# The probabilities of the first attention turned by VectorE and by transfers through DRAM, and its value product one iteration later

## The reference

```python
q_hk = (hidden_q @ Wq.T).reshape(b, s, H, K)
q_big = einsum('bshk,hkq->bshq', q_hk, w_kc_q)
kv_rope = kv_c * cos + rotate_half(kv_c) * sin
q_r = einsum('bshq,hqr->bhsr', q_big, W_qr)
k_r = einsum('bld,hdr->bhlr', kv_rope, W_kr)
attn = softmax(einsum('bhsr,bhlr->bhsl', q_r, k_r))
ctx_c = einsum('bhsl,bld->bhsd', attn, kv_rope)
ctx_lat = einsum('bhsd,hkd->bshk', ctx_c, w_kc_kv)
out = ctx_lat.reshape(b, s, H * K) @ Wo.T
x = x + tanh(g_xattn[0]) * out
```

## Time and profile before

| | |
|---|---|
| median of 3 runs | 1411.74 us (1410.79 to 1411.82) |
| the profiled execution | 1410.01 us |
| its span on the core | 1408.2 us |
| TensorE busy | 98% of the span |
| VectorE, ScalarE, GpSimd busy | 62%, 37%, 29% |
| transposes of `Pb` on TensorE | 256, from 41.7 to 461.4 us |

### The profile page before, as it was taken

One profiled execution on the slowest core, in us unless ns is written; L12 is line 12 of the kernel. 1 busy time (PEld: TensorE's weight loads), 2 busy tenths in 40 slices (PEclk: granted clock), 3 DMA queues, 4 the chain that ended last, 5 costly groups with the idle time before them and its releaser, 6 DMA issues.

```text
span 1408.2 us, 20791 instructions
## 1 busy us (share of the span) xinstructions
PE 1384.4 (98%) x7948; PEld 1128.5 (80%) x7948; DVE 874.9 (62%) x1729; ACT 519.2 (37%) x1599; POOL 404.9 (29%) x463
## 2 busy tenths in 40 slices
PE   6999999999999999999999999999999999999999
PEld 5888888888887788878887888778887788887887
DVE  5455454455554687777677757776788787734443
ACT  2544444444355322131113211321126777822221
POOL 3112322222224444111121112113527865621000
PEclk9999999999999999999999999999999999999999
DMA  5432010110203221111011101111214131132111
GB/s 202 150 108 89 33 66 8 53 39 8 83 24 94 86 74 56 47 31 49 23 38 42 46 17 48 41 45 49 79 50 141 49 128 61 47 113 67 53 46 45
DMA packets 65127, 89.07 MB, mean 63 GB/s; under 512 B 8044, under 2 KB 31724, under 8 KB 65028
## 3 DMA queue, kind: packets, MB, share of 16 engines
q1 hardware_dynamic: 65028, 87.74, 19.5%
HBM read 70.94 MB, written 16.78 MB: 62 GB/s over the span
## 4 chain that ended last, share of the span: by engine, by line
PE 92%; DVE 4%; POOL 1%; ACT 1%; DMA 1%; issue 0%; SPq 0%; DVEq 0%; ACTq 0%; POOLq 0%
PE bank L118 86%; PE bank L121 7%; DVE STG L130 0%; DVE AH L130 0%; DVE st L152 0%; DVE XR L140 0%; DMA STG<-in_WoT_dram 0%; DVE sm L146 0%; DMA XR<-in_x_dram 0%; ACT Pb L124 0%; ACT STG L124 0%; DVE XR L137 0%; POOL XR L137 0%; POOL P L130 0%; DVE MSK L136 0%
## 5 line engine op out<-in xcount | busy, mean ns | idle before, releaser
L118 PE MATMUL bank<-XT,AR 128*128 128x512 f32 x1152 | 280.2, 393 | 0.3 <-DVE AR L130 0.2
L118 PE MATMUL bank<-AR 128*128 128x512 f32 x1056 | 261.5, 397 | 0.9 <-DVE PTV L127 0.7
L118 PEld LDWEIGHTS bank<-XT,AR 128*128 128x128 f32 x1152 | 213.8, 188 | 48.5 <-issue 1.5
L118 PEld LDWEIGHTS bank<-AR 128*128 128x128 f32 x1056 | 193.4, 188 | 46.9 <-DVE PTV L140 2.5
L124 ACT ACTIVATE STG<-bank,b1c 128x512 f32<-128x512 f32 x128 | 88.4, 691 | 379.1 <-PE bank L118 300.6
L118 PE MATMUL bank<-AR,CT 128*128 128x512 f32 x768 | 190.3, 397 | 0.0
L118 PE MATMUL bank<-AR,AH 128*128 128x512 f32 x768 | 187.5, 391 | 0.0
L118 PEld LDWEIGHTS bank<-AR,AH 128*128 128x128 f32 x768 | 143.1, 188 | 30.3 <-issue 1.1
L118 PEld LDWEIGHTS bank<-AR,CT 128*128 128x128 f32 x768 | 142.7, 189 | 30.0 <-issue 0.4
L127 DVE CAST AH<-STG 128x512 fp32r<-128x512 f32 x192 | 91.0, 474 | 118.7 <-PE bank L118 104.4
L127 POOL CAST BA<-STG 128x256 fp32r<-128x256 f32 x64 | 29.6, 463 | 420.7 <-PE bank L118 312.5
(11 more groups left out here) (132 smaller groups left out, 1881.0 us busy)
## 6 DMA issues: line engine op xcount, KB each, us to landing
XR<-scr SPq DMA_DIRECT2D x52, 256.0 KB, 2.8
XR<-in_x_dram SPq DMA_DIRECT2D x32, 256.0 KB, 4.2
scr<-XR SPq DMA_DIRECT2D x32, 256.0 KB, 2.0
STG<-in_Wq_dram SPq DMA_DIRECT2D x8, 512.0 KB, 3.4
STG<-in_WoT_dram SPq DMA_DIRECT2D x8, 512.0 KB, 5.4
STG<-in_W1L_dram SPq DMA_DIRECT2D x16, 256.0 KB, 2.6
STG<-in_W_dram SPq DMA_DIRECT2D x16, 256.0 KB, 2.7
STG<-in_B1T_dram SPq DMA_DIRECT2D x64, 64.0 KB, 1.9
```

What stands on the lines that cost most here:

```text
L118: return self.e.matmul(o, w, x, start=start, stop=stop, skip_group_check=True) if self.e else Nothing()
```

## The change

For units 0 to 29 (`by_dma`), P is no longer turned by TensorE. VectorE transposes each 32 by 32 block of `Pb` within its own strip of 32 partitions and writes the blocks to `PY`, grouped by their place among the four block columns of a tile (`blocks1`, two instructions, ending in `py_ok`). SyncE stores `PY` to DRAM (`p_store`, 512 KB) and reads it back with rows and block columns exchanged in four transfers of 128 KB, in rows of 1 KB, into `PZ` (`p_load`). `split1p` makes the high part (ScalarE, one instruction of 1024 columns) and the low part (VectorE, one instruction, `pz_ok`) of `PT`. `PY` and `PZ` share their space with `TM`, which is used later.

The value product of a unit and both halves of its output product come one iteration later, up to iteration 31. Units 30 and 31 are still turned by TensorE, and the iterations 31 to 34 are written out so that the loop ends as before. The stores of x, `final1` and `kv_split` move one iteration back accordingly, and the four loads of x tiles per block are spread over p = 2, 3 and 4. In SyncE's queue `p_store(u - 2)` stands ahead of the weights' loads of iteration u and `p_load(u - 2)` behind them.

```diff
--- before.py
+++ after.py
@@ -159,6 +159,9 @@
         return self.e.max_index(o, m, x) if self.e else Nothing()
+
+    def turn(self, o, x):
+        return self.e.transpose(o, x) if self.e else Nothing()
     def memset(self, o, v):
@@ -223,6 +226,8 @@
         w12c = sb("w12c", [128, 2, 4], F32)
+        with ExitStack() as st1:
+            PYZ = sb("PYZ", [128, 2, 1024], F32, st1)
         TM = sb("TM", [128, 4, 512], FR, st12)
@@ -263,6 +268,7 @@
               for p in range(8)]
+        PY, PZ = PYZ[:, 0, :], PYZ[:, 1, :]
         sWq, sKq, sKc, sWo, sWr = STG[:, 0:1024], STG[:, 1024:1792], STG[:, 1792:2048], STG[:, 2048:3072], STG[:, 3072:3456]
@@ -295,6 +301,7 @@
         scr = [nc.dram_tensor(f"scr{k}", [NT, D], F32, kind="Internal").ap() for k in range(3)]
+        pscr = [nc.dram_tensor(f"pscr{k}", [128, 1024], F32, kind="Internal").ap() for k in range(2)]
         xs = [i["x"], scr[0], scr[1], scr[2], out]
@@ -326,6 +333,7 @@
         t_x4 = [sig(f"t_x4{k}", 16) for k in range(8)]
+        t_py, d_pz = sig("t_py", 16), sig("d_pz", 16)
         def kinds(count, names):
@@ -335,6 +343,7 @@
         ms2_ok, tl_ok2, tl_sum, al_in, ix_ok = kinds(on_dve, "ms2_ok tl_ok2 tl_sum al_in ix_ok")
+        py_ok, pz_ok = kinds(on_dve, "py_ok pz_ok")
         c_mh, c_sel, rs_ok, kvc_rd, kvr_ok, kvl_ok = kinds(on_pool, "c_mh c_sel rs_ok kvc_rd kvr_ok kvl_ok")
@@ -409,6 +418,17 @@
             return t_xf[tb][m]
+
+
+
+        def by_dma(u):
+            return u < 30
+
+        def blocks_in(t):
+            return t.rearrange("p (n i c) -> p n i c", i=4, c=32)
+
+        def blocks_out(t):
+            return t.rearrange("p (i n c) -> p n i c", i=4, c=32)
         def ct_read(u, half):
@@ -607,8 +627,11 @@
                     pe.wait_ge(*ps.free(key))
-                    pe.wait_ge(*ps.drained(("pt", u, 0)))
-                    pe.wait_ge(*ps.drained(("pt", u, 1)))
+                    if by_dma(u):
+                        pe.wait_ge(*pz_ok[u])
+                    else:
+                        pe.wait_ge(*ps.drained(("pt", u, 0)))
+                        pe.wait_ge(*ps.drained(("pt", u, 1)))
                     pe.wait_ge(*kvl_ok[m])
@@ -764,22 +787,35 @@
                     k1(u)
-                if u >= 3:
-                    wo1(u - 3, 1)
+                if 4 <= u < NU:
+                    wo1(u - 4, 1)
                 if u + 1 < 8:
                     prep_b(u + 1)
-                if 2 <= u <= NU + 1:
-                    pv1(u - 2)
+                if 3 <= u < NU:
+                    pv1(u - 3)
                 if u < NU and p == 7 and m + 1 < NM:
                     kv_turn(m + 1)
                 if u < NU and 3 <= p <= 6:
                     ln_turn(*after1(m), p - 3, ring4.next())
-                if 1 <= u <= NU:
-                    turn1(u - 1)
+                if 3 <= u < NU:
+                    wo1(u - 3, 0)
+                if u == 31:
+                    wo1(28, 1)
+                    pv1(29)
+                    turn1(30)
+                if u == 32:
+                    wo1(29, 0)
+                    wo1(29, 1)
+                    pv1(30)
+                    turn1(31)
+                    wo1(30, 0)
                 if u == 33:
+                    wo1(30, 1)
+                    pv1(31)
                     stA0(0)
-                if 2 <= u <= NU + 1:
-                    wo1(u - 2, 0)
+                    wo1(31, 0)
+                if u == 34:
+                    wo1(31, 1)
                 if u == 33:
@@ -1086,7 +1122,7 @@
                     if u:
-                        ac.wait_ge(*ps.full(("pt", u - 1, j)))
+                        ac.wait_ge(*(py_ok[u - 1, j] if by_dma(u - 1) else ps.full(("pt", u - 1, j))))
                     elif j == 0:
@@ -1108,6 +1144,13 @@
                     hi_of(key, CT[:, 512 * half:512 * half + 512], ps.ap(key)[:, :])
+
+            def split1p(u):
+                key = "pz", u
+                ac.wait_ge(*d_pz[u, 3])
+                if u:
+                    ac.wait_ge(*ps.full(("pv", u - 1, 1)))
+                hi_of(key, blocks_in(PT[:, 0:1024]), blocks_out(PZ))
             def turn1(u):
@@ -1188,13 +1231,19 @@
                     prep_b(u + 1)
-                if 2 <= u <= NU + 1:
-                    pv1(u - 2)
+                if 3 <= u < NU:
+                    pv1(u - 3)
                 if u < NU and p == 7 and m + 1 < NM:
                     kv_turn(m + 1)
                 if u < NU and 3 <= p <= 6:
                     ln_turn(*after1(m), p - 3)
-                if 1 <= u <= NU:
+                if 2 <= u < NU:
+                    split1p(u - 2)
+                if u == 31:
+                    pv1(29)
+                if u in (32, 33):
+                    pv1(u - 2)
+                if u in (31, 32):
                     turn1(u - 1)
@@ -1468,6 +1517,16 @@
                     lo_of(key, lo, ps.ap(key)[:, :], hi).then_inc(*ps.drain(key, on_dve))
+            def blocks1(u):
+                for j in range(2):
+                    e.wait_ge(*nm_ok[u, j])
+                    if u:
+                        e.wait_ge(*t_py[u - 1])
+                    e.turn(blocks_out(PY)[:, 4 * j:4 * j + 4], blocks_in(Pb)[:, 4 * j:4 * j + 4]).then_inc(*py_ok.mark((u, j)))
+
+            def split1p(u):
+                lo_of(("pz", u), blocks_in(PT[:, 1024:2048]), blocks_out(PZ), blocks_in(PT[:, 0:1024])).then_inc(*pz_ok.mark(u))
+
             def turn1(u):
@@ -1576,29 +1635,40 @@
                     k1(u)
-                if u >= 3 and (u - 3) % 8 == 7:
-                    final1((u - 3) // 8, 2)
-                    final1((u - 3) // 8, 3)
+                if 4 <= u < NU and (u - 4) % 8 == 7:
+                    final1((u - 4) // 8, 2)
+                    final1((u - 4) // 8, 3)
+                if u == 34:
+                    final1(3, 2)
+                    final1(3, 3)
                 if u + 1 < 8:
                     prep_b(u + 1)
-                if 2 <= u <= NU:
-                    pv1(u - 2)
+                if 3 <= u < NU:
+                    pv1(u - 3)
                 if u < NU and p == 7 and m + 1 < NM:
                     kv_turn(m + 1)
                 if u < NU and 3 <= p <= 6:
                     ln_turn(*after1(m), p - 3)
                 if u < NU and 2 <= p <= 5:
                     ln_pre(*after1(m), p - 2)
-                if 1 <= u <= NU:
+                if 2 <= u < NU:
+                    split1p(u - 2)
+                if 1 <= u < 31:
+                    blocks1(u - 1)
+                if u in (31, 32):
+                    pv1(u - 2)
                     turn1(u - 1)
                 if u == 33:
                     mask_turn(0)
                     masks_a(0)
                 if u == 34:
                     masks_b(0)
-                if 2 <= u <= NU + 1 and (u - 2) % 8 == 7:
-                    final1((u - 2) // 8, 0)
-                    final1((u - 2) // 8, 1)
+                if 3 <= u < NU and (u - 3) % 8 == 7:
+                    final1((u - 3) // 8, 0)
+                    final1((u - 3) // 8, 1)
+                if u == 33:
+                    final1(3, 0)
+                    final1(3, 1)
                 if u == 32:
@@ -1969,8 +2039,8 @@
                     norm1(u - 1)
-                if 2 <= u <= NU + 1 and (u - 2) % 8 == 7 and (u - 2) // 8 + 1 < NM:
-                    kv_split((u - 2) // 8 + 1)
+                if 3 <= u < NU and (u - 3) % 8 == 7 and (u - 3) // 8 + 1 < NM:
+                    kv_split((u - 3) // 8 + 1)
                 if u < NU and 2 <= p <= 5:
@@ -2081,6 +2151,20 @@
                 e.dma(sWo, i["WoT"][p]).then_inc(*d_Wo.mark(p))
+            def p_store(u):
+                e.wait_ge(*py_ok[u, 1])
+                if u >= 2:
+                    e.wait_ge(*d_pz[u - 2, 3])
+                e.dma(pscr[u % 2], PY).then_inc(*t_py.mark(u))
+
+            def p_load(u):
+                e.wait_ge(*t_py[u])
+                if u:
+                    e.wait_ge(*pz_ok[u - 1])
+                src = pscr[u % 2].rearrange("(j r) (i x) -> i r j x", j=4, i=4)
+                for k in range(4):
+                    e.dma(PZ[32 * k:32 * k + 32, :].rearrange("r (j x) -> r j x", j=4), src[k]).then_inc(*d_pz.mark((u, k)))
+
             def kv_load(m):
@@ -2121,18 +2205,21 @@
                 m, p = divmod(u, 8)
+                if 2 <= u < NU:
+                    p_store(u - 2)
                 if u + 1 < 8:
                     prep_a(u + 1)
                     prep_b(u + 1)
+                if 2 <= u < NU:
+                    p_load(u - 2)
                 if u >= 32:
                     ba_load(u - 32)
-                if u >= 3 and (u - 3) % 8 == 7 and u < NU:
+                if u < NU and 2 <= p <= 4:
+                    for tb in ((0,), (1, 2), (3,))[p - 2]:
+                        ln_load(*after1(m), tb)
+                if u >= 4 and (u - 4) % 8 == 7 and u < NU:
                     for b in (2, 3):
```

(10 more changed lines are left out.)

## The result

The changed kernel takes 1457.4 us (median of 4 runs, 1455.4 to 1459.9) against 1411.8 before: a ratio of 1.0321 [1.0301, 1.0342], slower. The profiled execution took 1455.4 us with a span of 1453.6, so 45.4 us more of span than before. The forecast was 1458.1.

A forecast was written before the change was run, and what follows sets the result against it. TensorE, busy 98% of the span, was taken to bound the kernel. The loop's -7.0, stalls of +43.9 and slower pace of +9.5 made +46.4 us: a median of 1458.1 us against 1411.7, range 1440 to 1474.

The forecast's parts named there:

- The stalls: TensorE waits five times, u = 2 to 6, for weights' loads queued behind the store of P; 43.9 us in all.
- L: Time from the issue of P's store to the landing of Wqr; taken as 5.8 us, a similar train having taken 6.15.
- My sign of waits of 8 to 11 us: TensorE's timeline would show five such waits ahead of `prep_a`'s 12 products, with 20 products after each at twice their time.
- nothing: In SyncE's queue, the loads of P behind `prep_b`'s loads have the long iteration and were to cost no time.
- The slow pace: TensorE at its slower clock after each stall: half of the start's 3.84 us, 1.9 us each, 9.5 in all.
- The eviction: TensorE waits for the value product's eviction, 0.85 us in bare iterations, 0.41 with another turn; 16.3 us come back.
- Turns, copy and difference: Per unit, VectorE's two block turns 1.4 us, ScalarE's copy 1.1 us and VectorE's difference 1.5 us.
- Its rival: P's round trip through DRAM becomes the bound, 0.8 us over in 24 iterations, +19 us: 1477; chance 0.13.
- The 0.8 us in iterations 11, 19 and 27: VectorE's sums of the residual make TensorE wait 0.8 us in each of these iterations, +2.4 us.
- the tail: At the loop's end TensorE's wait of 0.53 us for the normalised P of unit 31 goes, -0.5 us.
- The rival on the other side: The stalls ahead of `prep_a`'s products don't arise and -7.0 us stands: 1404.7 us; chance 0.04.
- The rule against the change: The skill gives full 128x128 transposes to TensorE; the change buys 0.83 us per unit with 1.4 us of VectorE and 1 MB.

The follow-up runs named there:

- e1: The changed kernel with SyncE's store of P put behind all the weights' loads of the iteration instead of ahead of them; 1414.95 us, 1.0027.
- e2: The changed kernel with SyncE's store of P put between the loads of `prep_a` and those of `prep_b`; 1430.9 us, 1.0153.
- e3: The changed kernel with TensorE kept multiplying in its five waits, 26 to 41 products whose result is overwritten; 1445.1 us, 1.0237.
- e11: e7 with P read back twice from unit 8 on: four loads, a wait for the last, the four again; 1489.2 us, 1.0549.
- e7: The changed kernel with SyncE issuing `prep_b(u + 1)`'s loads, store of P, `prep_a(u + 2)`'s loads, then load of P; 1411.6 us, 1.0008.
- e8: e7 with half of `wo1(u - 4, 1)`, six products, moved behind the value product as cover in 21 iterations; 1400.8 us, 0.9936.
- e4: e1 with TensorE's value product `pv1(u - 3)` put ahead of `wo1(u - 4, 1)` instead of behind it; 1419.3 us, 1.0055.
- e12: e8 with the load of the next block's first tile of x ahead of all else in SyncE's iteration 2; 1402.55 us, 0.9941.

## Why the prediction was right

- **The stalls: right in place and number, 6.6 us too long.** Five waits ahead of `prep_a`'s products: 7.3, 10.0, 6.6, 6.4, 7.0 = 37.3 us against 43.9 (8.7, 11.2 and 3 x 8.0). L was 4.6 to 5.3 us (44.39 to 48.94 the first time) where I took 5.8, the train's 6.15 brought down a little; five times 0.85 is 4.2 of the 6.6 us, and the shorter split and turns (below) are an estimated 1.6 more (0.1 at the first stall, 0.37 at the others). My sign of waits of 8 to 11 us was met by one of the five only. e1 and e2 show the mechanism, the place of a wait in SyncE's queue. e1 adds a second one that I named only as "nothing", `p_load`'s wait for the store.
- **The slow pace: right, and mis-sized.** 3.4, 3.75, 3.1, 3.3 and 3.0 us behind the five waits, by the groups' lengths against their normal ones, 16.6 us against 9.5; e3 takes 15.3 out. I had halved the 3.84 us between 13.87 and 17.71, but the slow stretch begins with the first 12 products and reaches into the XT,AR group: 1.3 + 0.9 + 1.1 us in those shown above. It is 28 products and a part of 12, not the 20 of my sign. My bound of 9.5 was no upper bound. The Trainium skill (TensorE: Matmul & The Clock Gate, Why this matters for your kernels) says that an idle gap costs the slower clock; the trace agrees, with a granted clock of 0.50 from 49 to 54 us.
- **The two errors cancel**: -6.6 and +7.1 us. The median came out within 0.7 us of the forecast for that reason, and that is luck; the sizes were not known so well.
- **The eviction: right.** The gain of a bare iteration was forecast as 0.84 - 0.85, that of one with a turn as 0.84 - 0.41 = 0.43. The scores before stand 12.60 and 12.98 us apart, after 12.57 to 12.60: some 0.02 and 0.40. The idle time printed is 0.70 and 0.26 us, as it counts from the modelled end of the group ahead; starts have to be compared with starts. Timeline of before, an iteration with the keys' turn and then a bare one:

```profile
128.45 1.16 PE L118 MATMUL bank<-K,Q 64*128 64x128 f32 x16
141.42 1.16 PE L118 MATMUL bank<-K,Q 64*128 64x128 f32 x16
154.02 1.16 PE L118 MATMUL bank<-K,Q 64*128 64x128 f32 x16
```

- **Turns, copy and difference** took 1.30, 1.05 and 1.23 us against 1.4, 1.1 and 1.5; the round trip was hidden, with about 1 us of room (e11). Its rival did not come true.
- **Two small terms were wrong.** The 0.8 us in iterations 11, 19 and 27 did not appear: VectorE's shorter split and turns (0.4 us) make up half of it, and the rest I did not trace. And the tail did not get shorter: the value product of unit 29 waits 1.45 us for PT, at 492.34. Everything besides stalls and pace came to 45.4 - 37.3 - 16.6 = -8.5 us, against -7.0.
- **The rival on the other side was priced too well.** Without the stalls I gave 1404.7; e7 is that kernel, at 1411.6, because iteration 2 then gets short, and VectorE's chain and the waits for WoT show. A stall hides what is shorter than itself.
- **The rule against the change** weighed rightly for a single turn, but its use is in what the turn covers: of the 25.2 us of transposes, some 16 came back as waits. Only with six products moved into that gap does the change win: e8 takes 10.8 us less than e7.

## What to carry to other kernels

A queue that is issued in order carries every wait to all that stands behind it (e1 and e2): for each instruction with a new wait, look for the next load that another engine is waiting for, and put it ahead. Before work is taken off the bounding engine, ask what it covers; a piece of independent work of just that size must take its place, since a larger one asks for its own inputs too early (e4). A long stall hides others, so a fix is to be priced from the trace without it.

## What the hardware did that I had not expected

- After a wait of 6.4 to 10 us TensorE was at the lower of its two clocks for some 7 us, and each time it cost 3.0 to 3.75 us on top. Shorter waits can do it. In e12 a wait of 2.17 us for WoT was followed by groups of 2.55, 3.51 and 2.77 us, in e8 one of 1.51 us by the normal 1.96, 1.89 and 1.50. Timeline of e12:

```profile
28.20 2.55 PE L118 MATMUL bank<-STG 128*128 128x512 f32 x4 [2.17 <-DMA STG<-in_WoT_dram]
30.54 3.51 PE L118 MATMUL bank<-Msb,STG 128*128 128x64 f32 x16
33.84 2.77 PE L118 MATMUL bank<-STG 128*128 128x64 f32 x12
```

- It makes the profiles differ by chance. Near the end of the first attention TensorE waits 1.39 us for the routing masks, in all kernels here, and in some of them 0.2 to 0.7 us shortly before (0.68 in before, none printed in after and e1). The clock of ten microseconds about there was 0.83 in the profiled run of before, 1.00 in that of after and 0.74 in that of e1. The 12 products AR,CT behind the masks took 3.0 us in six of the profiles and 4.5 to 5.5 in the other eight. From the last scores of the first attention to the end of the span, where the work is nearly the same, the profiles took 953.2 to 957.1 us. A difference of 2 or 3 us between two single profiles may be that alone. Runs of one kernel show it as well: the ten of e1 have mean clocks of 0.991 to 0.996 and times of 1412.65 to 1417.86 us, the lowest clock with the longest time. The first window here is of before, the second of e1:

```profile
474.53:484.53 10.00, 7.94 (x27) 5.36 (x27) 6.15 (x11) 2.46 (x5) 1.38 (x3) 0.83 0.36 124
```

```profile
477.16:487.16 10.00, 8.57 (x28) 5.89 (x27) 6.84 (x14) 1.70 (x3) 1.72 (x3) 0.74 0.25 82
```

- The granted clock reads 1.00 in the program's first 22 us although the groups there take twice as long (2.79 us for 12 products). There the durations have to be read, not the clock.
